# A pipelined transformer-like tower on one core: weights in fewer loads, the first gating in one go, and the moved slots of the first step

## What is computed

```python
h = einsum('bnk,dk->bnd', patches, W) + b                     # embedding, D = 64
xn = layernorm(h)
hid[t] = tanh(xn[t] @ W_ih.T + b_ih + b_hh + hid[t-1] @ W_hh.T)   # over the 16 images, one after the other
h = h + hid
x2 = layernorm(h)
logits = x2 @ gate_w + gate_b                                 # 16 experts
topk_vals, topk_idx = top_k(logits, 2); topk_w = softmax(topk_vals)
hx = relu(einsum('bsh,ehf->bsef', x2, w1) + b1)               # all experts, F = 128
y = x2 + sum_k topk_w[k] * (hx[topk_idx[k]] @ w2 + b2)
out = h + (y - mean(y)) / sqrt(var(y) + 1e-5) * gamma + beta
```

## Time and profile before

| | |
|---|---|
| median of 3 runs | 583.3 us (582.72 to 583.43) |
| the profiled execution's own time | 584.91 us |
| its span in the profile | 583.1 us |
| TensorE, busy | 534.7 us, 92% |
| VectorE, busy | 430.0 us, 74% |
| ScalarE, busy | 356.2 us, 61% |
| GpSimd, busy | 170.2 us, 29% |

### The profile page before, as it was taken

How to read it: one execution, slowest core, us unless ns; L and a number is a source line. 1 busy time by engine, 2 the same in 40 slices (tenths; PEclk the granted TensorE clock), 3 DMA queues, 4 the chain that set the end, 5 groups by cost and what they waited for, 6 DMA issues and landing times.

```text
span 583.1 us, 8948 instructions
## 1 busy us (share of the span) xinstructions
PE 534.7 (92%) x3138; PEld 358.0 (61%) x3138; DVE 430.0 (74%) x819; ACT 356.2 (61%) x596; POOL 170.2 (29%) x133
## 2 busy tenths in 40 slices
PE   2577999999999999999999999999999999999991
PEld 2365666576666767576666767576666657565640
DVE  1144868978787878978787888878787797886762
ACT  2236665767567674757667675757667475846561
POOL 4122011513132241513242241523232151311334
PEclk9999999999999999999999999999999899998996
DMA  3304683563819184562909174562809265462801
GB/s 79 95 15 107 146 191 75 137 145 74 194 31 233 32 181 101 125 156 63 203 22 229 46 177 105 121 161 65 203 18 219 60 142 125 107 146 71 184 0 42
DMA packets 30140, 67.45 MB, mean 116 GB/s; under 512 B 7056, under 2 KB 12432, under 8 KB 29968
## 3 DMA queue, kind: packets, MB, share of 16 engines
q1 hardware_dynamic: 30096, 66.89, 49.4%
HBM read 59.59 MB, written 7.28 MB: 115 GB/s over the span
## 4 chain that ended last, share of the span: by engine, by line
PE 78%; DVE 5%; ACT 5%; DMA 4%; issue 4%; POOL 2%; SPq 1%; POOLq 0%; DVEq 0%; ACTq 0%
PE pZ L711 29%; PE pO L724 28%; PE pA L660 4%; PE pA L735 4%; PE pB L635 4%; DMA xcur<-x_in 4%; ACT hexp L426 2%; PE pA L653 2%; PE pB L686 2%; PE pA L645 2%; PE pA L675 1%; DVE acc L559 1%; POOL inv_std L327 1%; SPq L293 1%; PE pB L695 1%
## 5 line engine op out<-in xcount | busy, mean ns | idle before, releaser
L426 ACT ACTIVATE hexp<-pZ,b1c 128x784 f32<-128x784 f32 x256 | 229.5, 908 | 83.1 <-PE pZ L711 80.9
L543 DVE SCALAR_TENSOR_TENSOR prod<-pO,b2c,spread 128x392 f32<-128x392 f32 x256 | 151.6, 623 | 98.4 <-PE pO L724 91.8
L724 PE MATMUL pO<-hexp,w2s 128*64 128x392 f32 x1024 | 199.8, 506 | 1.3 <-ACT hexp L426 1.3
L711 PE MATMUL pZ<-xt,w1hi 128*128 128x392 f32 x512 | 194.8, 380 | 3.7 <-ACT hexp L426 2.3
L711 PE MATMUL pZ<-xt,w1lo 128*128 128x392 f32 x512 | 175.7, 343 | 0.0
L711 PEld LDWEIGHTS pZ<-xt,w1hi 128*128 128x128 f32 x512 | 97.5, 190 | 64.1 <-issue 36.2
L327 POOL TENSOR_TENSOR inv_std<-var,nhalf 112x7 f32<-112x7 f32 x48 | 74.7, 1566 | 174.5 <-DVE var L477 174.5
L724 PEld LDWEIGHTS pO<-hexp,w2s 128*64 128x64 f32 x1024 | 70.4, 137 | 79.2 <-issue 63.9
L559 DVE TENSOR_TENSOR acc<-acc,prod 128x784 f32<-128x784 f32 x112 | 118.4, 1057 | 0.1
L711 PEld LDWEIGHTS pZ<-xt,w1lo 128*128 128x128 f32 x512 | 97.9, 191 | 0.0
L334 POOL TENSOR_TENSOR h2b<-h2c,bet 112x448 f32<-112x448 f32 x16 | 20.2, 1263 | 169.0 <-DMA h2c<-h_dram 169.0
(11 more groups left out here) (74 smaller groups left out, 425.6 us busy)
## 6 DMA issues: line engine op xcount, KB each, us to landing
spread<-gates_dram SPq DMA_DIRECT2D x128, 392.0 KB, 9.0
h_dram<-h SPq DMA_DIRECT2D x16, 199.1 KB, 2.5
h2c<-h_dram SPq DMA_DIRECT2D x16, 199.1 KB, 9.7
xcur<-x_in SPq DMA_DIRECT2D x16, 196.0 KB, 9.9
out<-yo SPq DMA_DIRECT2D x16, 196.0 KB, 9.3
w1f<-w SPq DMA_DIRECT2D x2, 512.0 KB, 6.1
w2s<-w SPq DMA_DIRECT2D x1, 512.0 KB, 6.8
gates_dram<-gt SPq DMA_DIRECT2D x16, 28.0 KB, 2.0
```

What stands on the lines that cost most here:

```text
L426: nc.scalar.activation(hexp[u % RING][:, :].rearrange("p (b c) -> p b c", b=2), halves(pZ[u % 2]), ACT.Relu, bias=b1c[:, u:u + 1])\
L543: nc.vector.scalar_tensor_tensor(out=prod[q % RING][:, b * HALF:(b + 1) * HALF], in0=halves(pO)[:, b, :], scalar=b2c[:, q:q + 1], in1=spre ...
L711: last = nc.tensor.matmul(halves(pZ[e % 2])[:, b, :], w[:, e, :], xt[par][:, b * HALF:(b + 1) * HALF], start=(k == 0), stop=(k == 1))
L724: last = nc.tensor.matmul(halves(pO)[k * D:(k + 1) * D, b, :], w2s[:, e, :], hexp[e % RING][:, b * HALF:(b + 1) * HALF], start=True, stop= ...
```

## The change

The loads: the embedding's weights and bias come as one array, the cell's weights as one, the two biases as one, `gate_w` already doubled. The host only lays the arrays out. w1's two halves are loaded right behind the cell's, and wait with the gate's on a semaphore of their own, `gate_loaded`. ScalarE makes w1hi in the prologue, VectorE makes w1lo in slot 1 of body -2; GpSimd has no part in it.

The slots: `at(t, steady, first=..., fill=...)` gives the fill's slot for t < 0, the first's for t = 0 and the steady one for t > 0. In bodies -2 and -1 the embedding's `embed_in` moves behind `hidden_turn`; in body -1 the logits move ahead of `embed_turn`, `find_second` and `gate_weights` follow `find_first` at once, exp stands ahead of the tanh, and `gates_turn` ahead of `hidden_turn`. In body 0 nearly all work that is not the experts' moves back: `x2_turn` from slot 1 to 5, `embed_turn` 2 to 6, logits and `recur` 3 to 7, `hidden_turn` and `embed_in` 5 to 9, `find_second` 5 to 9, `gate_weights` 7 to 11, `gates_turn` 10 to 13, and the closing operations of the layer norms by one to three slots. The steady bodies are as before.

```diff
-        cell_loads, expert_loads = [], []
-        for k in range(2):
-            rows = slice(k * D, (k + 1) * D)
-            cell_loads += [(cell[rows, k, :], w_ih), (cell[rows, 1 - k, :], w_hh),
-                           (rbias[rows, 0:1], b_ih.unsqueeze(1)), (rbias[rows, 1:2], b_hh.unsqueeze(1)),
-                           (gwf[rows, :], gate_w)]
-            expert_loads += [(w1f[rows, :, :], w1)]
+        embed_loads = [(tokt[:, :], tok)]
+        cell_loads = [(cell[:, :, :], cell_w), (rbias[:, :], cell_b)]
+        gate_loads = [(w1f[0:D, :, :], w1), (w1f[D:2 * D, :, :], w1), (gwf[:, :], gate_w),
+                      (gbias[:, :], gate_b.partition_broadcast(P))]
...
-                if known(t, 0) and gate:
-                    pool.wait_ge(w1_split, 1)
-                    nc.gpsimd.tensor_tensor(w1lo[:, :, :], w1f[:, :, :], w1hi[:, :, :].bitcast(f32), ALU.subtract)\
-                        .then_inc(w1_split, 1)
...
-                    if embed and u == (3 if known(t, -1) else 5):
+                    if embed and u == at(t, 5, first=9):
                         keep_h1(t + 3, 1 - par)
...
-                    if gate and u == 6:
+                    if gate and u == at(t, 6, first=10, fill=2):
                         GATE.wait(act, t + 1, "diff")
...
-            act.wait_ge(cell_loaded, CELL_LOADED)
+            act.wait_ge(gate_loaded, GATE_LOADED)
+            nc.scalar.activation(w1hi[:, :, :], w1f[:, :, :], ACT.Copy).then_inc(w1_split, 1)
...
+                    if known(t, -1) and u == 1:
+                        dve.wait_ge(w1_split, 1)
+                        nc.vector.tensor_tensor(w1lo[:, :, :], w1f[:, :, :], w1hi[:, :, :].bitcast(f32), ALU.subtract)\
+                            .then_inc(w1_split, 1)
...
+                    if gate and known(t, 0) and u == 4:
+                        find_second(g)
+                        gate_weights(g)
...
-                    if gate and u == 7:
+                    if gate and not known(t, 0) and u == at(t, 7, first=11):
                         gate_weights(g)
...
-                    if gate and u == 3:
+                    if gate and u == at(t, 3, first=7, fill=2):
                         logits(t + 1, 1 - par)
-                    if mix and u == 3:
+                    if mix and u == at(t, 3, first=7):
                         recur(t + 2)
-                    if gate and u == 10:
-                        gates_turn(t + 1, embed, close)
+                    if gate and u == at(t, 10, first=13, fill=4):
+                        gates_turn(t + 1, embed and not known(t, 0))
...
-                    if gate and u == 1:
+                    if gate and u == at(t, 1, first=5):
                         x2_turn(t + 1)
```

More of the change, by code:

```diff
@@ L29, in vit_tower_kernel @@
     X = mybir.AxisListType.X
-    D = w_ih.shape[0]
+    D = cell_w.shape[2]
     STEPS = out.shape[0]
@@ L39, in vit_tower_kernel @@
     F = w1.shape[2]
-    K_IN = tok_w.shape[1]
+    K_IN = tok.shape[1] - 1
     PAIRS = (TILES + 1) // 2
@@ L145, in vit_tower_kernel, with at @@
         CLOSE = Chain("close_stage", "turned center square var rstd norm gamma out")
-        def after(t, fill, steady):
-            return fill if known(t, 0) else steady
+        def at(t, steady, first=None, fill=None):
+            slot = fill if known(t, 0) else first if known(t, 1) else None
+            return steady if slot is None else slot
         embed_loaded = sem("embed_weights_loaded")
-        cell_loaded = sem("cell_and_gate_weights_loaded")
+        cell_loaded = sem("cell_weights_loaded")
+        gate_loaded = sem("w1_and_gate_weights_loaded")
         experts_loaded = sem("expert_weights_loaded")
@@ L293, in _ @@
                 sp.dma_start(dst, src).then_inc(cell_loaded, 16)
+            for dst, src in gate_loads:
+                sp.dma_start(dst, src).then_inc(gate_loaded, 16)
             run(sp, body)
@@ L447, in body @@
                         nc.scalar.activation(gt[:, :], pB[0:2 * E, 0:FIRST], ACT.Copy).then_inc(GATE.sem, 1)
-                    if mix and u == 7:
+                    if mix and u == at(t, 7, first=10):
                         square(MIX, t + 2, "h2", 1, h2[:, :, 0:D])
@@ L452, in body @@
                         square(CLOSE, t - 1, "center", 2, cen[:, :, :])
-                    if embed and u == 9:
+                    if embed and u == at(t, 9, first=11):
                         square(EMBED, t + 3, "kept", 0, h1[1 - par][:, :, 0:D])
@@ L456, in body @@
                         close_norm(t - 1)
-                    if mix and u == 12:
+                    if mix and u == at(t, 12, first=14):
                         MIX.wait(act, t + 2, "x2")
@@ L583, in body @@
                             .then_inc(MIX.sem, 1)
-                    if gate and u == 5:
+                    if gate and not known(t, 0) and u == at(t, 5, first=9):
                         find_second(g)
-                    if gate and u == 7:
+                    if gate and not known(t, 0) and u == at(t, 7, first=11):
                         gate_weights(g)
-                    if mix and u == 9:
+                    if mix and u == at(t, 9, first=11):
                         norm_var(MIX, s, 1)
@@ L591, in body @@
                         norm_var(CLOSE, c, 2)
-                    if embed and u == 11:
+                    if embed and u == at(t, 11, first=12, fill=15):
                         norm_var(EMBED, a, 0)
-                    if mix and u == 12:
+                    if mix and u == at(t, 12, first=13):
                         norm_scale(MIX, s, 1, x2[:, :, :], h2[:, :, 0:D])
-                    if mix and u == 14:
+                    if mix and u == at(t, 14, first=15):
                         MIX.wait(dve, s, "hi")
@@ L630, in embed_in @@
                 if not known(s, 2):
-                    GATE.wait(pe, s - 2, "biased")
+                    GATE.wait(pe, s - 2, "gt" if known(s, 3) else "biased")
                 elif not known(s, 1):
@@ L688, in logits, with gates_turn @@
                 last.then_inc(GATE.sem, 1)
-            def gates_turn(s, embed, close):
+            def gates_turn(s, embed):
                 GATE.wait(pe, s, "gates")
@@ L753, in body @@
                             second_layer(t - 1, Q - 1)
-                    if mix and u == after(t, 4, 5):
+                    if mix and u == at(t, 5, first=9):
                         hidden_turn(t + 2)
-                    if embed and u == (3 if known(t, -1) else 5):
+                    if embed and u == at(t, 5, first=9):
                         embed_in(t + 3)
@@ L759, in body @@
                         sum_turn(t - 1, 1 - par, mix)
-                    if gate and u == 1:
+                    if gate and u == at(t, 1, first=5):
                         x2_turn(t + 1)
-                    if mix and u == 2:
+                    if mix and u == at(t, 2, first=6):
                         embed_turn(t + 2)
```

33 lines of the change are left out of this document (18 added, 15 removed).

## The result

| | before | after |
|---|---|---|
| median | 583.4 us (582.7 to 584.5, 4 runs) | 590.9 us (589.1 to 591.1, 4 runs) |
| ratio, 95% interval | | 1.012 (1.0095 to 1.0145) |
| profiled execution, its span | 584.9, 583.1 | 591.1, 589.4 |

The account below looks back on a forecast made before the run. TensorE bounds the steady bodies, the chain from engine to engine the fill. Terms -1.4 + 0.7 + 0.1 + 1.6 + 1.9 + 2.95 sum to +5.9 us, forecasting 589.2 us, range 585.0 to 592.0.

Parts of the forecast that it names:

- (7): Body 0: TensorE waits at least 1.3 us at the turn of the gates, now in slot 13; taken as +1.9.
- (8): Body 1: step 4's load of xcur, issued behind the spread loads, comes late, so `embed_in` waits 2.95 us.
- rival D: Body 1: waits as forecast, and the clock falls while TensorE stands at `embed_in`: +7.5, 590.8 us; chance 0.22.
- C: Fill: the clock is up from the first joined stretch at 17 us: -3.0, 580.3 us; chance 0.1, later 0.12.
- (1): Prologue: fewer small loads let the chain reach xn at 11.2 us, a gain of 1.4.
- (3): Body -1: logits start at 32.5 instead of 34.95, gates come at 38.2, and `hit` takes 0.28, not 2.84.
- (4): Body -1: `hidden_turn` goes behind the gates' turn, the square stays behind `keep_h1`; 0.85 gained, first relu at 49.6.
- (5): Body 0: third expert starts 1.4 us earlier, 0.7 of TensorE's work comes later, 0.1 in slots 2 and 3; net -0.6.
- (6): Body 0: third and fourth experts and part of the first `second_layer` run at the low clock: +1.6; bounds 0 and 2.9.
- A: Fill: the clock rises earlier, as TensorE works without a gap from 38.2 to 47.65: +3.1, 586.4 us; chance 0.2.
- B: Body 1: the load of step 4 arrives in time as spread loads drain quicker: 586.2 us; chance 0.08.
- (2): Body -2: with `embed_in` behind the tanh and `hidden_turn`, the square moves from 25.37 to about 23.6: gain 1.8.

Follow-up runs that it names:

- the load ahead: Changed kernel with SyncE's load of xcur for step 4 moved ahead of the spread loads of step 1: 584.5 us, 1.003 of before.
- the kernel with the experts held back: Changed kernel with body 0's slots put back and the first expert's matmuls waiting for the row sum of step 1: 582.0 us, 0.9971 of before.

## Why the prediction was right, and where its sizes were off

Slower, as forecast, by the mechanism of terms (7) and (8), and with rival D behind it (590.8 forecast, 590.9 measured). That the two agree so closely is luck in part, since several terms are off with opposite signs. (C stands with 0.1 in its own paragraph and with 0.12 in the numbers, which add up to one with the latter.)

- Terms (1) to (3), the prologue, body -2 and the gating: xn at 11.39 (11.2), the square at 23.45 (23.6), the logits at 32.30 (32.5), gates' turn at 38.09 (38.2). The loads held nothing, and `hit` took 0.28. Right.
- Term (4): mis-sized, 1.7 gained and not 0.85. `hidden_turn` starts 0.72 behind the turn and not 0.9, and I took the row's 2.88 as the time until the next matmul starts, while groups of fourteen follow each other at 2.5 to 2.6 (38.81, 41.34, 43.92): the end of a group overlaps the start of the next.
- Terms (5) and (6): right in their sizes. The third expert starts 0.95 behind the first relu, after 2.82 of idle time (2.9), and the eight matmuls come every 0.33. The low level cost about 1.4 (1.6): 1.2 for the eight, and 1.72 for the first `second_layer` where the same form takes 1.54.
- Term (7): 1.30 of wait, the lower bound that I worked out, and not 1.9. The 0.6 that I added for VectorE being late did not come.
- Term (8): the mechanism is right, and the load ahead shows it to be most of the loss. It was mis-sized: gt comes 3.92 ahead of body 1 (3.95), but the landing took 14.1 and not 12.9 (14.2 and 13.5 in two experiments), so the wait is 4.12 and not 2.95. One row of one transfer was taken as a constant.
- Rival D: it happened, and cost 2.8, not 1.6. I priced two experts and a part of a `second_layer` at the low level, and left out `embed_in` itself, 1.34 more.
- Rivals A and C, the early clock: excluded by the 0.53 at 52.15. TensorE worked without a gap from 38.09 to 46.88, and the next matmuls still ran low. B: excluded by the 14.1.
- The signs: the gates' wait (1.30 of 1.2 to 2) and the wait for xcur came as named; the first relu at 48.75 is earlier than the 49.3 to 50 that was to show it right, which is term (4) again.
- The sum: up to body 1 the terms gave +2.9, measured 1.0; the wait and the clock behind it, 4.55 with D, measured 6.9.
- "Of the 9 us by which the gates come earlier, 8 hang on nothing" was too kind. The experiments put the new order of the fill at a loss of 3.8 against the old one with the same loads, and the gain of the fill is all the loads'. And the gain that was to be had there, the square behind the copy, I had named as the reason in terms (2) and (4) without asking what it was worth: 3.9 us in the changed kernel, 4.2 on the loads alone together with the move of `embed_in`.

## What to carry to other kernels

When an operation is moved to a later slot, list every transfer that is issued behind its output on the same queue, and not only those that carry it: here a load with 0.75 us of room stood behind eight that waited for the moved one, and cost more than all that moved. A load that hangs on nothing belongs ahead of those that do. And in a fill, ask of each operation of the chain what stands ahead of it in its own engine's queue: one copy behind the square instead of ahead of it was worth about 4 us, where the whole reordering of the fill lost 3.8. Work that stands between two waits can be what covers the second: the turns and logits of body 0 did so for the arrival of the gates.

## What the runs showed of the hardware

- **The granted clock falls in a wait, and stays low through busy time**: it falls in the wait of 4.12 and is still 0.50 from 102 to 104 us with TensorE busy for 2.00 of 2.00, 4 us after the wait. In the kernel before it is 0.50 at 457 us as well, with TensorE busy throughout. TensorE's last recorded idle time ahead of that is a short one, for the same load in body 12:

```profile
455.38 1.59 PE L635 MATMUL pB<-tokw,xcur 65*112 65x65 f32 x14 [0.34 <-DMA xcur<-x_in]
```

  In the kernel with the experts held back it fell at 457 us too, behind a wait of 0.99 for that load. But 0.25 at 159 us passed without a fall, and a wait of 1.5 for a relu near 525 us is followed by the low level in before and not in the changed kernel. So whether a short wait is the cause is not shown.
- **When the clock rises differs between executions of the same work**: 392 columns take 0.34 at 49.92 in one and 0.53 at 52.88 in another. In the records the time goes with the mean granted clock: of the 29 runs of before beside the first experiments, the 16 at 0.991 and 0.992 average 582.0, the 4 at 0.985 and 0.986 585.7. These 3.7 us are about as much as any effect of the fill here, and three runs that lie within 0.7 us of each other don't show them.
- **A load behind eight others of one queue**: the load of step 4, issued right behind the 8 spread loads, lands 12.9 to 14.2 us from its issue in before, the change, the moved slots alone and the gates in slot 15. The four loads of xcur that stand ahead of it in before land in 3.1 to 3.6, and the load of step 4 in 3.5 where it is issued ahead of the spread loads.
